# A transformer sandwich on one core: where the rounded and the full activation come from

## The reference

```python
# attention
qkv = x_norm @ W_qkv.T ; attn = softmax(q * 128**-0.5 @ k.T) ; out = attn @ v
x = x + layernorm(out)
# feed-forward on layernorm(x); hidden size 512; tlin(x, w, s) = (x @ w.T) * s, w in {-1, 0, 1}
h = silu(tlin(h0, w1, s1)) * tlin(h0, w2, s2)
h = gelu(tlin(h, h1, s_h1), approximate=False)
h = gelu(tlin(h, h2, s_h2), approximate=False)
x = x + layernorm(tlin(h, w3, s3))
```

## Time and profile before

| what | value |
|---|---|
| runs | 163.35, 163.86, 164.72 us; median 163.86 |
| profiled execution, first to last instruction (span) | 160.3 us |
| time around the span (median less span) | 3.56 us |
| busy: PE, DVE, ACT, POOL | 137.1, 123.2, 90.7, 81.1 us |
| mean granted TensorE clock | 0.987 of full |

### The profile page before, as it was taken

The page is one execution under the profiler, slowest core; times in us unless marked ns, Lnnn a source line. Parts: engine busy times, 40 slices in busy tenths (PEclk is TensorE's granted clock), DMA queues, the critical chain, the costliest instruction groups (busy, mean ns, idle before and its releaser), DMA issues. The chain is left out here.

```text
span 160.3 us, 2214 instructions
## 1 busy us (share of the span) xinstructions
PE 137.1 (86%) x676; PEld 102.1 (64%) x676; DVE 123.2 (77%) x337; ACT 90.7 (57%) x157; POOL 81.1 (51%) x73
## 2 busy tenths in 40 slices
PE   6996859868999799999998979999978598979850
PEld 2564636345768587687886847869766385856740
DVE  1777678938979989689769796894697788695864
ACT  3057677455998345847875428678834555463420
POOL 3249339905424846363275672632948745273521
PEclk9999997799999999999999999999999999999999
DMA  4997000000000000000000010000000100001001
GB/s 141 267 359 265 0 4 2 0 0 0 2 0 4 0 0 0 0 4 2 0 0 4 2 65 0 0 4 0 0 0 7 60 6 0 0 0 65 4 0 65
DMA packets 3837, 5.35 MB, mean 33 GB/s; under 512 B 368, under 2 KB 2544, under 8 KB 3824
## 3 DMA queue, kind: packets, MB, share of 16 engines
q1 hardware_dynamic: 3824, 5.19, 9.7%
HBM read 4.14 MB, written 1.05 MB: 32 GB/s over the span
## 5 line engine op out<-in xcount | busy, mean ns | idle before, releaser
L203 POOL TENSOR_TENSOR a_lo<-act_full,a_hi 128x512 fp32r<-128x512 f32 x34 | 45.4, 1343 | 35.6 <-DVE a_hi L523 29.7
L699 PE MATMUL F<-a_hi,h_hi 128*128 128x512 f32 (+1 forms) x128 | 36.3, 405 | 4.8 <-DVE a_hi L523 4.5
L312 ACT ACTIVATE act_full<-F,sc 128x512 f32<-128x512 f32 x31 | 21.0, 689 | 26.2 <-PE F L709 26.2
L523 DVE CAST a_hi<-act_full 128x512 fp32r<-128x512 f32 x47 | 28.3, 609 | 7.4 <-ACT act_full L312 6.4
L709 PE MATMUL F<-a_lo,h_hi 128*128 128x512 f32 (+1 forms) x128 | 33.5, 392 | 0.4 <-DVE a_lo L433 0.4
L699 PEld LDWEIGHTS F<-a_hi,h_hi 128*128 128x128 f32 x128 | 22.3, 189 | 12.1 <-DVE a_hi L523 8.0
L198 POOL TENSOR_TENSOR rstd<-ve,minus_half 128x4 f32<-128x4 f32 x15 | 15.8, 1055 | 24.7 <-DVE ve L557 8.9
L709 PEld LDWEIGHTS F<-a_lo,h_hi 128*128 128x128 f32 x128 | 23.7, 188 | 6.3 <-DVE a_lo L433 0.8
L859 PE MATMUL F<-warm 128*128 128x512 bf16 x50 | 15.8, 467 | 1.9 <-POOL warm L188 1.3
L515 DVE SCALAR_TENSOR_TENSOR act_full<-F,sc,silu 128x512 f32<-128x512 f32 x16 | 11.9, 746 | 5.1 <-ACT silu L306 5.1
L306 ACT ACTIVATE silu<-F,sc 128x512 f32<-128x512 f32 x16 | 10.8, 689 | 6.4 <-PE F L709 6.3
(11 more groups left out here) (120 smaller groups left out, 244.2 us busy)
## 6 DMA issues: line engine op xcount, KB each, us to landing
h_raw<-h SPq DMA_DIRECT2D x2, 1024.0 KB, 8.9
xs<-x SPq DMA_DIRECT2D x4, 256.0 KB, 6.3
out<-outs SPq DMA_DIRECT2D x3, 256.0 KB, 2.1
w_raw<-w SPq DMA_DIRECT2D x1, 512.0 KB, 5.4
w_raw<-w SPq DMA_DIRECT2D x1, 256.0 KB, 9.9
out<-outs SPq DMA_DIRECT2D x2, 128.0 KB, 1.7
wa_raw<-w_attn SPq DMA_DIRECT2D x1, 192.0 KB, 2.7
sc<-scales SPq DMA_DIRECT2D x1, 8.5 KB, 5.1
```

The source lines that it names most:

```text
L203: nc.gpsimd.tensor_tensor(dst[:, o, :], act_full[:, o, :], hi[:, o, :].bitcast(f32), ALU.subtract).then_inc(done, 1)
L312: nc.scalar.activation(act_full[:, o, :], F[o][:, :], ACT.Gelu, scale=sc[:, first_scale + o:first_scale + o + 1]).then_inc(done, 1)
L523: nc.vector.tensor_copy(hi[:, o, :], act_full[:, o, :]).then_inc(hi_sem, 1)
L699: nc.tensor.matmul(out, terms[k][0], terms[k][2], start=(k == 0), stop=False)
```

## The change

ACT evaluates Gelu twice from the same PSUM bank: first into the fp32r hi tile, then into act_full. The first one waits for the product, and for slice 0 of each block also until the readers of the hi tile of the block before are through (`hi_free`); the wait for the slot of act_full stands behind it. DVE's casts of a2 and a3 are taken out, those of the last block's halves (L538) too; the a1 casts stay. The semaphores a2_hi_ready and a3_hi_ready are now raised by ACT.

```diff
-            def gelu(b, o, first_scale, in_psum, slot_free, done):
+            def gelu(b, o, first_scale, in_psum, hi, hi_free, hi_done, slot_free, done):
+                scale = sc[:, first_scale + o:first_scale + o + 1]
                 act.wait_ge(in_psum, KT * b + o + 1)
+                if b > 0 and o == 0:
+                    act.wait_ge(*hi_free)
+                nc.scalar.activation(hi[:, o, :], F[o][:, :], ACT.Gelu, scale=scale).then_inc(hi_done, 1)
                 act.wait_ge(*slot_free)
-                nc.scalar.activation(act_full[:, o, :], F[o][:, :], ACT.Gelu,
-                                     scale=sc[:, first_scale + o:first_scale + o + 1]).then_inc(done, 1)
+                nc.scalar.activation(act_full[:, o, :], F[o][:, :], ACT.Gelu, scale=scale).then_inc(done, 1)
 
             def gelu1(b, o):
-                gelu(b, o, S_H1, h1_in_psum, a1_lo_done(b, o), a2_full)
+                gelu(b, o, S_H1, h1_in_psum, a2_hi, (h2_in_psum, KT * b), a2_hi_ready, a1_lo_done(b, o), a2_full)
 
             def gelu2(b, o):
-                gelu(b, o, S_H2, h2_in_psum, a2_lo_done(b, o), a3_full)
+                gelu(b, o, S_H2, h2_in_psum, a3_hi, (yT_in_psum, b), a3_hi_ready, a2_lo_done(b, o), a3_full)
...
                 act.wait_ge(h2_in_psum, KT * BLOCKS + g)
+                nc.scalar.activation(a3_hi[:, KT - 1, c], (F[3], A[3])[g][:, c], ACT.Gelu,
+                                     scale=sc[:, S_H2 + KT - 1:S_H2 + KT]).then_inc(a3_hi_ready, 1)
                 if g == 0:
                     act.wait_ge(*a2_lo_done(LAST, KT - 1))
...
             def a2_parts(b, o):
-                act_hi(b, o, a2_hi, a2_full, a2_hi_ready, h2_in_psum, KT * b)
...
             def a3_parts(b, o):
-                act_hi(b, o, a3_hi, a3_full, a3_hi_ready, yT_in_psum, b)
...
                 dve.wait_ge(a3_full, n)
-                nc.vector.tensor_copy(a3_hi[:, o, c], act_full[:, o, c]).then_inc(a3_hi_ready, 1)
                 lo_part(a3_lo[:, o, c], act_full[:, o, c], a3_hi[:, o, c], a3_hi_ready, n, a3_lo_dve)
```

## The result

| | before | changed |
|---|---|---|
| runs, us | 162.17 to 164.72, median 163.61 | 169.15 to 172.45, median 171.45 |
| ratio changed / before, 95% interval | | 1.037 [1.029, 1.044] |
| span of the profiled execution, us | 160.3 | 170.6 |
| mean granted TensorE clock in it | 0.987 | 0.920 |

The change makes the kernel slower by 3.7%. The four executions of the changed kernel differ by how long the clock was down (mean clock 0.945 in the shortest, 0.920 in the two longest, of which the profiled one is one), and the ratio leaves the two longest out; 1.037 x 163.61 is 169.7 us. On another chip the ratio was 1.034 [1.027, 1.041] (run e9).

What follows compares the result with a forecast made beforehand. PE, busy 137.1 of 160.3 us, was taken as nearly the bound. +3.5 us without the clock and +1.3 for the clock make +4.8 on 163.86: 168.7 us, 2.9% slower, range 164.0 to 171.0.

Steps and rivals of the forecast that it cites:

- What goes, and what PE gets: 31 of 47 casts at L523 go; PE's pauses for a2_hi end, worth -1.9 us in the last block.
- What ACT pays: 33 more activations bring ACT to some 112 us busy; bank F[3] charged 0.1 us in each of two blocks.
- POOL set free, DVE pays: POOL's a3_lo runs unbroken; DVE's xn2 takes 3.99, 5.1, 5.1 us; blocks 0 to 2 cost +1.45, +1.85, +2.1 us.
- The sum without the clock: Over all four blocks: 1.45 + 1.85 + 2.1 - 1.9 = +3.5 us.
- The clock: PE's longer pauses at xn2 lower its granted clock: one fall, after block 2, +1.3 us.
- rival 3: Tiles of xn2 held up, with clock falls after blocks 1 and 2: 170.2 us, chance 0.14.
- The base: Median 163.86 us lies 3.56 above the profiled span of 160.3, taken as unchanged time outside it.
- A sign that I read wrongly: POOL's idle time before L203 would fall from 29.7 to under 18 us.
- Rival 1: DVE's xn2 tiles slip in between two POOL instructions, so the relief wins: -2.4 us, 161.5 us, chance 0.13.
- rival 2: Tiles of xn2 held up by POOL, without a fall of the clock: 167.4 us, chance 0.25.
- rival 4: At xn2 the lock costs half, +3.5 less some 3 us: about 164.4 us, chance 0.10.
- the lock: At xn2, each ready POOL instruction holds up one DVE tile, at 1.3 us a tile.

Runs made afterwards that it cites:

- e9: The changed kernel measured once more, in the same rounds as e10: 170.71 us, ratio 1.034 to the kernel before.
- e4: The changed kernel with four unread matmuls on zeros behind each of the first three xn2 transposes of blocks 1 to 3: 165.96 us, ratio 1.013.
- e1: The changed kernel with POOL waiting for the next block's four xn2 tiles before a3_lo slices 1 and 2: 161.35 us, ratio 0.982.
- e2: The changed kernel with POOL waiting for the next block's four xn2 tiles before last_add and all of a3_lo: 154.6 us, ratio 0.944.
- e6: The kernel before, casts kept, with a second Gelu into an unread spare tile ahead of each Gelu: 167.04 us, ratio 1.010 [0.997, 1.024].
- e10: The kernel of e2 measured again, with more rounds: 154.77 us, ratio 0.939 to the kernel before.
- e8: The changed kernel with POOL waiting for xn2 before the three a3_lo instructions, but not before last_add: 158.03 us, ratio 0.962.
- e7: The kernel before with POOL waiting for the next block's four xn2 tiles before last_add and a3_lo: 160.81 us, ratio 0.983.

## Why the prediction was right, point by point

The direction and the path that leads to it were right. The size came near in part by luck: the term of the clock was too small and the base too high.

- **What goes, and what PE gets.** Right. In the last block the three pauses of the earlier trace rows are gone: h2's 8 hi matmuls run on from 154.62 without a wait, and last_down follows at once. Timeline of PE, after:

```profile
154.62 2.03 PE L701 MATMUL F<-a_hi,h_hi 128*128 128x512 f32 x8
156.49 2.03 PE L711 MATMUL F<-a_lo,h_hi 128*128 128x512 f32 x8
...
162.10 0.63 PE L701 MATMUL A<-a_hi,w_hi 128*128 128x256 f32 x4
```

  The term of -1.9 us was too small, though: 2.7 measured, after and in e4. I had added the idle times of the rows. From the first of h2's hi matmuls to h2's third slice it was 141.66 to 147.19 before and 154.62 to 158.35 after, 1.80 us less for listed pauses of 1.27. A stop costs more than the idle time in its row, since running matmuls start every 0.23 us but each takes 0.4 to its end, and the idle time is counted from that end.
- **What ACT pays.** Right in kind: ACT went to 107.3 us (I said 112; I had added the full 0.69 us of each Gelu and not the pitch of 0.58), and the bank F[3] is now what the second up slice waits for, 0.4 us in blocks 0 and 1 of e1 and e2, where PE had waited 0.27 us for x2T_lo. e6 bounds ScalarE's cost by 2.4%, but no run isolates the two or three tenths that I charged.
- **POOL set free, DVE pays.** Right, the step that decides. Counted from the landmarks, xn2 starts 0.54 and 0.29 us earlier in blocks 0 and 1 and 0.13 later in block 2, as forecast (0.65 and 0.4 earlier, 0.1 later). Forecast 3.99, 5.1 and 5.1 us for xn2, measured 3.93, 4.88 and 4.89. I took a POOL instruction at 1.28 us; back to back they follow every 1.22. For PE I had +1.45, +1.85 and +2.1 us; e4 shows 2.14 (some 1.5 without its own matmuls), 1.78 and 2.05.
- **The sum without the clock.** Forecast +3.5, in e4 +3.2 us of span, some 2.5 without its added matmuls in block 0. The gains at the end were taken at 1.9 and came to 2.7.
- **The clock.** The mechanism was right, the term was mis-sized. I took one fall and +1.3 us. The changed kernel falls behind all three places, and its blocks 0 to 2 take 0.8, 2.0 and 2.9 us longer than those of e4, together 5.7. In e9's trace they take 1.2, 1.7 and 2.4 us longer, together 5.3, and by the ratios (1.037 and 1.034 against e4's 1.013) it is 3.4 to 3.9 us. I had priced a fall by the row of the start phase, 4 us at 0.57. Behind block 1 the clock is low for 6.8 us between 96 and 108 us, mostly beside busy matmuls. And I had argued the fall from the length of the rest, which e2 and e10 show isn't all that decides. My own rival 3, falls in more than one place, came nearer. Against the ratio of 1.037 the forecast of 2.9% is low by 0.8 points; the median of 171.45 lies just above my range.
- **The base.** I put 3.56 us around the span. The changed kernel has 172.45 - 170.6 = 1.85, and the kernel before an execution of 162.17 us that fits its span of 160.3 with 1.87. So the profiled execution was the fastest, not the median, and what I added to the median should have been added to 162.2. That gives 167.0 us: the base hid 1.7 us of what the clock's term lacked.
- **A sign that I read wrongly.** I said that POOL's idle time before L203 would fall under 18 us. It rose to 35.7 (with all releasers from 35.6 to 46.1): in a longer block POOL, done sooner with a3_lo, waits longer for a1. The sign should have been the idle time at a3_lo alone, which is gone in blocks 0 to 2.
- **The rivals.** Rival 1 (the tiles slip in between) is excluded by the scale of e2, e8, e1 and the changed kernel, rival 2 (no fall of the clock) by the stretches, rival 4 (half the lock) by three full stretches of xn2. The advice of the Trainium skill, "Perfetto Trace Analysis", section "Optimizing Scalar/DVE Operations", to move work to ACT when DVE is saturated, is worth 4% here (e2 over e7), with DVE busy for 77% of the span, but only after POOL is held.

## What to carry to other kernels

An instruction that seems to be only late work can be the brake that keeps two other engines apart. Before taking it away, look at who waits for it, what that engine will do as soon as it may, and whether that holds up instructions on the critical path; then hold it with a wait of its own if need be. A wait on an engine with idle time cost almost nothing here (one weight load of PE, 0.6 us) and was worth 9%. Where TensorE must rest, count the clock too: here it cost 3.4 to 5.7 us, next to some 5.4 for the lock (1.5 + 1.8 + 2.1).

## What the runs showed that I had not expected

- On these tiles DVE and POOL take turns strictly. One small DVE instruction (a 128x128 tile that takes some 0.25 us when free) waits for a whole 128x512 POOL instruction each time, however many POOL has ready; 0 to 4 of them make 1.1, 2.0, 2.95, 3.93, 4.89 us.
- The clock fell from 2.4 to 1.2 GHz while PE did single 128x128 transposes every 1.22 us (0.63 in 132 to 136 us of the changed kernel, with three of them). With four 128x512 matmuls after each of the first three it stayed at 1.00 (e4), and these fillers, whose result nobody reads, won 3.4 to 5.7 us.
- The clock stayed low longer than the row of the start phase suggested: in the changed kernel it was at 0.50 for a whole stretch of 4 us in which PE was always busy (100 to 104 us), and for 6.8 and 10.2 us in all behind blocks 1 and 2.
- The kernel with the same waits may keep the clock in one execution and lose it in another: e2 and e10 are the same kernel, at a mean of 0.985 and 0.973.
